# Head attention with q and k packed in four pieces and x loaded a sequence ahead, and the layers' row norm on ScalarE as a scale and a shift

## What is computed

```python
q = (x @ Wq.T + bq).reshape(B, S, H, D)          # B=16, S=512, H=16, D=16
scores = jnp.einsum('bqnd,bknd->bnqk', q, k) / sqrt(D)
attn = jax.nn.softmax(scores, axis=1)            # over the heads, per query and key
x = _layernorm(x + out @ Wo.T + bo)
...
def _layer(x, ...):                              # two of these
    h = shift_token(x)                           # half of the columns come from the row before
    q, k, v = jnp.split(h @ wqkv, 3, axis=-1)    # 8 heads of 64
    ...                                          # l2norm, rotary, window of 128 + 128 keys
    x = x + o @ wo
    h = shift_token(x)
    h = (h - mu) / jnp.sqrt(var + 1e-05) * lg + lb
    a, g = jnp.split(h @ w1 + b1, 2, axis=-1)
    return x + (a * gelu(g)) @ w2 + b2
x = _layernorm(x + _L0_ffn_ref(x, ...))
```

## Time and profile before

| | |
|---|---|
| median of 3 runs | 4712.84 us (4704.44 to 4716.74) |
| the profiled execution: its own time, and its span | 4714.33 us, 4712.5 us |
| PE, PEld busy | 92%, 76% |
| DVE, ACT, POOL busy | 70%, 55%, 50% |
| head attention | from 0 to about 1690 us of the span |
| layers | from about 1700 us to the end |

### The profile page before, as it was taken

One profiled execution on the slowest core, in us unless ns is written; L12 is line 12 of the kernel. 1 busy time (PEld: TensorE's weight loads), 2 busy tenths in 40 slices (PEclk: granted clock), 3 DMA queues, 4 the chain that ended last, 5 costly groups with the idle time before them and its releaser, 6 DMA issues.

```text
span 4712.5 us, 99362 instructions
## 1 busy us (share of the span) xinstructions
PE 4314.1 (92%) x36928; PEld 3584.7 (76%) x36928; DVE 3282.6 (70%) x6004; ACT 2597.2 (55%) x5984; POOL 2372.1 (50%) x1655
## 2 busy tenths in 40 slices
PE   5888888888889869999999999999999999999998
PEld 3666666666666647888888888888888888888887
DVE  3887888888888856666566656656666666666665
ACT  2444444444444436666666666666666666666664
POOL 3887888887888843333333333333333333333332
PEclk8999999999999989999999999999999999999999
DMA  4444334444334310000000000000000000000000
GB/s 84 65 62 64 53 53 58 64 63 64 53 53 57 42 47 22 15 18 15 16 18 15 13 16 17 15 25 15 22 20 20 23 20 22 18 26 20 20 20 25
DMA packets 138238, 160.03 MB, mean 34 GB/s; under 512 B 18079, under 2 KB 103926, under 8 KB 137718
## 3 DMA queue, kind: packets, MB, share of 16 engines
q1 hardware_dynamic: 137718, 153.02, 18.4%
HBM read 52.31 MB, written 25.17 MB: 16 GB/s over the span
## 4 chain that ended last, share of the span: by engine, by line
PE 40%; issue 9%; DVE 8%; ACT 3%; POOL 3%; SPq 0%; DVEq 0%; DMA 0%; POOLq 0%; ACTq 0%
PE b_X L1364 8%; PE b_M L1409 7%; PE b_F L1435 6%; PE b_M L1487 4%; PE b_F L1514 3%; PE b_S L1389 3%; PE b_S L1398 2%; ACT b_p L1123 2%; PE b_S L1380 2%; PE b_M L1478 1%; DVE b_hn L1222 1%; POOL b_rn L955 1%; PE b_X L1346 1%; DVE b_ss L1149 1%; DVE b_mx L1170 1%
## 5 line engine op out<-in xcount | busy, mean ns | idle before, releaser
L319 ACT ACTIVATE a_p<-a_S 128x512 f32<-128x512 f32 x1024 | 529.4, 603 | 700.0 <-PE a_S L504 700.0
L371 DVE TENSOR_REDUCE a_nm<-a_S 128x128 fp32r<-128x2048 f32 x256 | 586.4, 2291 | 228.3 <-PE a_S L494 187.8
L1123 ACT ACTIVATE b_p<-b_S,b_nb,b_rn 128x256 f32<-128x256 f32 (+1 forms) x1024 | 536.7, 534 | 224.2 <-DVE b_nb L1173 223.4
L1364 PE MATMUL b_X<-b_wqkv,b_hT 128*128 128x512 f32 x2304 | 650.4, 418 | 1.4 <-DVE b_hT L1197 1.4
L248 POOL TENSOR_TENSOR a_z<-a_p 128x1024 f32<-128x1024 f32 x256 | 603.7, 2358 | 85.4 <-ACT a_p L319 84.5
L1435 PE MATMUL b_F<-b_hnT,b_w 128*114 128x256 f32 (+1 forms) x4608 | 632.2, 287 | 5.7 <-issue 5.7
L1435 PEld LDWEIGHTS b_F<-b_hnT,b_w 128*114 128x114 f32 (+1 forms) x4608 | 576.7, 178 | 19.2 <-issue 5.9
L948 POOL TENSOR_TENSOR b_t<-b_t 128x512 f32<-128x512 f32 x128 | 165.4, 1292 | 829.7 <-DVE b_t L1147 829.7
L256 POOL TENSOR_TENSOR a_p<-a_p,a_zi 128x640 f32<-128x640 f32 x256 | 397.4, 1552 | 216.4 <-DVE a_zi L397 216.2
L1182 DVE TENSOR_SCALAR b_a<-b_F,w_b 114x256 f32<-114x256 f32 (+1 forms) x384 | 183.7, 478 | 432.6 <-ACT b_g L1044 432.6
L1364 PEld LDWEIGHTS b_X<-b_wqkv,b_hT 128*128 128x128 f32 x2304 | 418.4, 190 | 84.8 <-DVE b_hT L1197 1.8
(11 more groups left out here) (142 smaller groups left out, 8934.9 us busy)
## 6 DMA issues: line engine op xcount, KB each, us to landing
a_q<-a_parts SPq DMA_DIRECT2D x128, 256.0 KB, 10.1
a_k<-a_parts SPq DMA_DIRECT2D x128, 256.0 KB, 10.7
a_x<-in_x SPq DMA_DIRECT2D x16, 512.0 KB, 15.3
a_xr<-in_x SPq DMA_DIRECT2D x64, 128.0 KB, 3.1
x_after_heads<-a_n SPq DMA_DIRECT2D x64, 128.0 KB, 2.3
b_x<-x_after_heads SPq DMA_DIRECT2D x16, 512.0 KB, 4.1
x_after_layer<-b_xo SPq DMA_DIRECT2D x32, 256.0 KB, 2.3
b_x<-x_after_layer SPq DMA_DIRECT2D x16, 512.0 KB, 3.9
```

Of the source, the lines that this page charges most:

```text
L319: nc.scalar.activation(probs[u % NE][:, hs], S[:, hs], ACT.Exp, scale=HDIM ** -0.5).then_inc(s_exp, 1)
L371: nc.vector.tensor_reduce(out=negmax[u % 2][:], in_=S[:].rearrange("p h q -> p q h"), axis=AX.X, op=ALU.max, negate=True).then_inc(s_nm, 1)
L1123: last = nc.scalar.activation(probs[hf][:, i, keys(w_)], SB[:, i, keys(w_)], ACT.Exp, bias=nb[hf][:, i:i + 1], scale=rn[w_ % 2][:, h:h + 1 ...
L1364: last = nc.tensor.matmul(X[i][:], hT_of(k, a), wqkv[:, b, k, i * INNER:(i + 1) * INNER], start=(k == 0 and (a, b) == PART_PAIRS[0]), stop ...
```

## The change

Head attention: `pack` copies one piece of 128 channels, and runs in units 4, 7, 10 and 12 (`PACK_AT`), again as eight DMAs, each with half of the bytes; q and k have a semaphore each. x for sequence n + 2 is loaded in unit 2 of sequence n (`X_AT`), after x of n + 1 has been transposed in unit 0; x of sequence 1 is loaded during the start. The residual rows of query tile qt are loaded in unit 4 qt + 3 instead of 4 qt + 6. The loop now covers 12 sequences instead of 14, the others are written out. Layers: VectorE makes only shift = -mean * rstd (one column), and ScalarE writes `hn` as x * rstd + shift in two instructions, ahead of its evacuation of q.

```diff
-    PACK_AT = (READY_AT[1] + 2, READY_AT[3] + 2)
+    PACK_AT = tuple(u + 2 for u in READY_AT)
+    X_AT = 2
...
-        with engine.Fori(0, (SEQS - 2) // 2) as i:
+        with engine.Fori(0, (SEQS - 4) // 2) as i:
...
-        def pack(n, par, which):
-            sp.wait_ge(s_part, part_count(n, CT * which + CT - 1, 2))
+        def pack(n, par, i):
+            which, ot = divmod(i, CT)
+            sp.wait_ge(s_part, part_count(n, i, 2))
             for t, (of_k, of_q) in enumerate(TERMS):
                 part = of_k if which else of_q
-                sp.dma_start(qk8[par][which][16 * t:16 * t + 16], parts[which][:, part]).then_inc(s_pack[par], 16)
+                sp.dma_start(qk8[par][which][16 * t:16 * t + 16, :, ot], parts[which][:, part, ot]
+                             ).then_inc(s_pack[par][which], 16)
...
-        pack(0, 0, 0)
-        pack(0, 0, 1)
+        sp.wait_ge(s_pt, CT)
+        load_x(1)
+        for i in range(4):
+            pack(0, 0, i)
         def one(n, par, r):
             for u in units_of(n):
-                if u == 0 and exists(n) and exists(n + 1):
-                    sp.wait_ge(s_pt, 8 * n + CT)
-                    load_x(n + 1)
-                nn, back, uu = lagged(n, u, 3, UNITS)
-                if uu % TILES == TILES - 1 and exists(nn):
-                    load_rows(nn, uu // TILES)
+                if u == X_AT and exists(n) and exists(n + 2):
+                    sp.wait_ge(s_pt, 8 * (n + 1) + CT)
+                    load_x(n + 2)
+                if u % TILES == TILES - 1 and exists(n):
+                    load_rows(n, u // TILES)
...
+        def layernorm(t, p, w2_, par2):
+            act.wait_ge(s_lsh, t + 1)
+            need(act, s_hT, t + 3)
+            for dst, src in ((hn[:, 0:P], x2[par2][:, w2_, 0:P]), (hn[:, P:CH], hs[:, w2_])):
+                last = nc.scalar.activation(dst, src, ACT.Identity, bias=shift[p][:, 0:1], scale=rstd[p][:, 0:1])
+            last.then_inc(s_hn, 1)
...
                     dve.wait_ge(s_rs, T - 1)
-                    need(dve, s_hT, T + 1)
-                    nc.vector.tensor_scalar(hn[:, 0:P], x2[p2][:, w2_, 0:P], mv[p][:, 0:1], rstd[p][:, 0:1],
-                                            ALU.subtract, ALU.mult)
-                    nc.vector.tensor_scalar(hn[:, P:CH], hs[:, w2_], mv[p][:, 0:1], rstd[p][:, 0:1],
-                                            ALU.subtract, ALU.mult).then_inc(s_hn, 1)
+                    need(dve, s_hn, T - 3)
+                    nc.vector.tensor_scalar(shift[p][:, 0:1], mv[p][:, 0:1], rstd[p][:, 0:1], -1.0,
+                                            ALU.mult, ALU.mult).then_inc(s_lsh, 1)
```

More of the change, by code:

```diff
@@ L110, in head_attention @@
     s_vv = sem("v_evacuated")
-    s_pack = [sem(f"packed{i}") for i in range(2)]
+    s_pack = [[sem(f"packed_{n}{i}") for n in "qk"] for i in range(2)]
     s_S = sem("scores")
@@ L149, in sequences @@
         one(0, 0, 0)
-        with engine.Fori(0, (SEQS - 2) // 2) as i:
+        with engine.Fori(0, (SEQS - 4) // 2) as i:
             one(2 * i + 1, 1, i)
             one(2 * i + 2, 0, i + 1)
-        one(SEQS - 1, 1, SEQS // 2 - 1)
-        one(SEQS, 0, SEQS // 2)
+        for n in range(SEQS - 3, SEQS + 1):
+            one(n, n % 2, n // 2)
     def part_count(n, i, part):
@@ L488, in scores_bank @@
             if u == 0 and b == 0:
-                pe.wait_ge(s_pack[par], PACKED * (r + 1))
+                for of in s_pack[par]:
+                    pe.wait_ge(of, PACKED * (r + 1))
             qt, kt = u // TILES, u % TILES
@@ L737, in layers @@
     stats = sb("stats", [P, 2, 6])
-    mv, ve, rstd = ([sb(f"{n}{i}", [P, 2]) for i in range(2)] for n in ("mv", "ve", "rstd"))
+    mv, ve, rstd, shift = ([sb(f"{n}{i}", [P, 2]) for i in range(2)] for n in ("mv", "ve", "rstd", "shift"))
     hn = sb("hn", [P, CH])
@@ L793, in layers @@
     s_rs = sem("ln_rstd")
+    s_lsh = sem("ln_shift")
     s_hn = sem("ln_normed")
@@ L1068, in one @@
                 live, feed = tile_exists(T), seq_exists(n - 1)
+                if tile_exists(T - 2):
+                    layernorm(T - 2, p, (w_ - 2) % TILES, par if w_ >= 2 else 1 - par)
                 if live:
@@ L1217, in one @@
                 if tile_exists(T - 2):
-                    n2, w2_ = back(n, w_, 2)
-                    p2 = par if w_ >= 2 else 1 - par
                     dve.wait_ge(s_rs, T - 1)
-                    need(dve, s_hT, T + 1)
-                    nc.vector.tensor_scalar(hn[:, 0:P], x2[p2][:, w2_, 0:P], mv[p][:, 0:1], rstd[p][:, 0:1],
-                                            ALU.subtract, ALU.mult)
-                    nc.vector.tensor_scalar(hn[:, P:CH], hs[:, w2_], mv[p][:, 0:1], rstd[p][:, 0:1],
-                                            ALU.subtract, ALU.mult).then_inc(s_hn, 1)
+                    need(dve, s_hn, T - 3)
+                    nc.vector.tensor_scalar(shift[p][:, 0:1], mv[p][:, 0:1], rstd[p][:, 0:1], -1.0,
+                                            ALU.mult, ALU.mult).then_inc(s_lsh, 1)
                 if live:
```

## The result

The changed kernel takes **4571.8 us** (median of 4 runs, 4568.7 to 4574.8), the kernel before 4710.6 (4 runs, 4704.4 to 4716.7): ratio 0.9705, 95% interval 0.9689 to 0.9722.

A forecast was written before the change was run, and what follows sets the result against it. TensorE was taken to work nearly all the time, so its waits were priced: 98 + 3 + 2 + 3 + 24 = 130 us off the profiled 4714.33, median 1.5 lower: 4583 us. Own range 4565 to 4602; over the cases 4545 to 4632.

The forecast's parts named there:

- The boundary: Head attention, 15 changes of sequence: TensorE's stall for the k pack goes, 6.5 us each, 98 us; bounds 72 and 108.
- rival (a): Head packs: a piece takes as long as a pair does now; about 4810 us; chance 5%.
- rival (e): Changes of sequence: only the idle time is saved, another wait taking its place; 4609 us; chance 10%.
- The start: Start of head attention: the first q piece flows from about 27 instead of 29.5; 3 us, between 0 and 5.
- Unit 0, units 10 and 11, and the rest: Head stage: x earlier, rows at other units, shorter loop; together 2 us, between -10 and +10.
- Tiles w_ = 3: Layers: projection L1364 moves up by 0.87 of the 1.04 us wait for `hn`; 24 us.
- w_ = 1: Layers: ScalarE's later q gives most of the gain back; 0.1 us saved in 32 tiles, 3 us.
- rival (b): Layers: the shift waits for GpSimd as L1222 does; 48 us lost, 4658 us; chance 4%.
- One sign: Layers, tiles w_ = 1: projection L1364 would wait for VectorE's low half of the transposed rows instead of `hn`.
- Even tiles: Layers: ScalarE 0.33 us later, covered by 0.66 us; no loss, without cover 20 us.
- (c): Layers give nothing, as ScalarE's later q and k delay scores or projections; 4610 us; chance 18%.
- (d): Layers: all of the wait goes and more, ScalarE's pair at the short bound; about 4550 us; chance 10%.

The follow-up runs named there:

- Experiment 9: The changed kernel, but each piece waits for the last part of its pair, as the pairs did: 4673.9 us.
- early (5): The kernel before with the packs in pieces, each two units after its projection, and nothing else changed: 4598.6 us.
- (before, 2): The layers' edit alone (norm as scale and shift on ScalarE), with the head stage of the kernel before: 4695.0 us.
- number 8: The changed kernel without any loop, norm on VectorE as before, GpSimd's product held back until the odd tile's norm is done: 4455.8 us.
- number 4: The changed kernel with the head loop and both layers' loops written out, so no loop at all: 4490.8 us.
- number 10: number 4 (ScalarE's norm, no loop) with GpSimd's product held back until the norm is done: 4496.3 us.
- Experiments 7: number 4 with the layers' norm of the kernel before, on VectorE: 4524.4 us.
- experiment 1: The head edits alone, with the layers of the kernel before: 4598.2 us.
- experiment 3: The changed kernel with all 17 passes of the head stage written out, layers' loops kept: 4519.6 us.

## Why the prediction was right, and where its sizes were off

**The boundary (98 predicted, 96.5 measured).** Right in mechanism: by bytes, not by number of transfers. The prediction gave k's second piece 3.9 + 8.3 = 12.2 us from its first issue; measured are 415.7 + 6.4 - 411.24 = 10.9, so it lands at 422.1, 4.1 us before the scores begin at 426.17. The step came out at 5.71 us against 463.6 - 457.66 = 5.94. That is 7.0 less than the mean of 12.72 before at ten ends; the five at a jump back of the loop take 7.27 to 7.63 (mean 7.44), which the term did not have. So 98 against 96.5 is partly luck: ten ends gave 0.5 us more than the 6.5 reckoned, and five gave 1.2 less. Experiment 9 shows that when the pieces go is what matters; rival (a) falls with its 1.06 us per transfer, rival (e) with the 5.71. One limit was added up wrongly: half packs could take at most (460.07 - 434.1 - 3.9) / 2 = 11.0 us of flow, not 11.4; each took 10.9 in all from issue to landing, so about 7 of flow. The Trainium skill, SBUF — State Buffer, section "The DMA setup-cost knee", has a fixed charge of about 2 us per transfer. It does not add up in turn for transfers queued one behind another: those of 128 KB landed 1.06 us apart here.

**The start (3 predicted, 9.4 measured).** The step "the weight loads still hold the DMA engines ... until 25" was wrong: it made a mean share of 0.62 over 8 us into 5 us of full use followed by none. The first q piece was issued at 22.40, 6 us before the first pair, and flowed beside the weights. The scores start at 56.50:

```profile
22.40 10.42 SPq L200 DMA_DIRECT2D a_q<-a_parts  x16
...
56.50 1.86 PE L497 MATMUL a_S<-a_q,a_k 128*128 128x128 bf16 x16 [17.89 <-DMA a_k<-a_parts]
```

The window from 20 to 28 moves 299 GB/s where it moved 215, and the share goes from 0.62 to 1.00: the engines had room for both. This term also scatters: in the traces of eleven kernels whose pieces are not held, the first subtraction comes at 55.0 to 66.3 us, with no cause that I can name; against 70.1 before, 4 to 15 us is what can be said.

**Unit 0, units 10 and 11, and the rest (2 predicted, 22.0 measured).** Two parts. Units 10 and 11 of even sequences stalled in before beside the q pack, TensorE's waits having this line (seven of the eight lie in unit 10, of sequences 2, 4, ... 14), which has no counterpart after:

```profile
PE a_O L521 <- issue: 13.9, 8, 2.1
```

I had seen no reason for that to change and did not price it. It is gone in every kernel with pieces, early (5) or held (9), and there in both with pairs (before, 2). Whether the 256 KB transfers cause it, or only where the code lies, no run separates. The other part, 4.0 + 2.3 = 6.3 us in unit 0 and the rest, stands against the 2 predicted.

**Tiles w_ = 3 (24 predicted, 23.1) and w_ = 1 (3, 2.7).** Right, with their working: the pair on ScalarE spans 3699.23 to 3700.12, 0.89 us against 0.86 assumed; the shift takes 0.21, so rival (b) falls. The point that in w_ = 1 ScalarE's late q gives the gain back is shown by number 8 beside number 4: the norm stays on VectorE, q is evacuated 0.69 us into the tile instead of 2.28 (medians), and the tiles w_ = 1 lose another 10.0 (355.8 to 345.8) and 17.1 us (370.7 to 353.6). It is not the held product, for number 10, which has it with ScalarE's norm, stays at 355.7 and 370.8. One sign did not come: TensorE was to wait for the low half of the transposed rows, but its new wait is the one for `o_n`, 0.24 us a tile, which stands just ahead of them in the same chain behind ScalarE's q; number 8 does not have it. And `hn` still waits 0.36 us in tiles w_ = 1 of the second layer, not 0.2. The Trainium skill, SBUF — State Buffer, section "Who interferes with whom", names `tensor_scalar` as an instruction that can lock the port pair shared with GpSimd, if its operands meet conditions. Experiments 7 and 8 agree for 128 columns from SBUF (1.55 against 0.34 us); the shift of one column (0.21 us) was not held up.

**Even tiles (0 predicted, -1.0 in w_ = 2, -6.3 in w_ = 0).** The cover named for ScalarE's delay held: in the medians of tiles w_ = 0 and 2, q is evacuated 0.77 us later, and the low half of the rows is done when it was. The 6.3 is no matter of the norm: experiment 1, with VectorE's norm, has 19.2 less in the first layer and 23.2 more in the second, the changed kernel 16.1 less and 22.3 more. The prediction allowed "a different layout of the code" 10 us either way under the head's term; it struck in the layers. So the 27 of the layers became 18, and rivals (c) and (d) both fall.

**In sum:** 130 predicted, 139 by medians and 145.7 by the two spans, which is what the terms add up to. The start (+6), units 10 and 11 (+16), unit 0 and the rest (+4) against the boundary (-1.5), w_ = 0 and 2 (-7), w_ = 1 and 3 (-1), less 0.7 by which the layers as a whole gain less than their tiles. The mechanisms were right; that the total came so near is partly luck. Two effects that I had not priced, the stalls of units 10 and 11 that went and those of the layers' w_ = 0 that moved, are of opposite sign and partly hid each other, and the surplus of the start lies within its own scatter.

**What stays open:** what sets the place of the layers' stalls (they move when the code ahead of them is another; how is not known), and the end of the stalls in units 10 and 11. Not tried was whether GpSimd's product of number 8 could start beside the instructions that read PSUM even later or earlier, nor any change to the start, where TensorE still waits 18.3 us for k in number 8.

## What to carry to other kernels

A transfer that waits for the last part of its data should be cut where its data are cut, if the engines are busy through it: here time went by bytes, and the first half was then free. When one engine's instruction waits out another's, first try to hold the other back, before moving work to a third engine that has a queue of its own: one wait was worth 69 us here, the move 34. And when steps that do the same differ in a trace with "issue" as the reason, look for the loop's jump, and write the loop out, or make its pass longer, before tuning anything else: all loops together were worth 81 us here, more than half as much as the whole change.

## What the runs showed of the hardware that was not expected

- A jump back of the head loop costs 1.7 us in the unit before it and 3.7 in the one after (means of five in the changed kernel), 5.5 in all, and this did not grow when the pass had twice the instructions (5 jumps 27 us, 2 jumps 11).
- In a loop the units took 5.53 us, written out 5.50.
- The layers' loops lost 27, 34 or 15 us (before, changed kernel, experiment 3) with the same code in the loops and other code ahead of them.
- The delay of VectorE by GpSimd was seen for `tensor_scalar` from SBUF to SBUF only: with the product beside it, `tensor_scalar` of 128 columns went from 0.34 to 1.55 us, while a one-column one (0.21) and the subtraction with one operand in PSUM (0.69) were not touched.
